# The state scan of a decoder layer laid out as 4 states x 32 channels on the partitions, with one scan instruction for a pair of rows and four sum strips

## The reference, cut to what matters

```
A  = -exp(A_log)                                   # 2048 x 16
dA = exp(dt_t[..., None] * A)                      # b, d, n
dBx = dt_t[..., None] * B_t[:, None, :] * x_t[..., None]
h  = dA * h + dBx
y  = einsum('bdn,bn->bd', h, C_t)
...
y  = (ys + D_param[None, :, None] * xc) * silu(z)
```

## Time and profile before

| what | value |
|---|---|
| median of 3 runs | 3586.15 us (3581.65 to 3586.78) |
| the profiled execution | 3582.83 us |
| its span, first to last instruction | 3581.5 us |
| the scan's DVE work | 446.3 to 1251.3 us of the span |
| DVE busy in that stretch | 791.2 of 804.9 us |
| POOL busy | 739.7 us |
| PE busy | 612.5 us |
| ACT busy | 358.2 us |
| mean granted TensorE clock in it | 0.95 |

### The profile page before, as it was taken

How to read it: one execution, slowest core, us unless ns; L and a number is a source line. 1 busy time by engine, 2 the same in 40 slices (tenths; PEclk the granted TensorE clock), 3 DMA queues, 4 the chain that set the end, 5 groups by cost and what they waited for, 6 DMA issues and landing times. The chain is left out here.

```text
span 3581.5 us, 41307 instructions
## 1 busy us (share of the span) xinstructions
PE 3221.2 (90%) x12763; PEld 2387.8 (67%) x12763; DVE 2195.0 (61%) x1925; ACT 1512.5 (42%) x2148; POOL 1399.2 (39%) x794
## 2 busy tenths in 40 slices
PE   9999777878777689999799999997889999999996
PEld 7877433333332267898587878786668888888884
DVE  6554499999999946621377777774644333333426
ACT  4447644444444432411387888782321122121111
POOL 0002299999999823000287878780100000000001
PEclk9999889999999999999899999999999999999998
DMA  3124531113110076422211111115211111111101
GB/s 110 41 80 165 184 128 62 45 50 139 50 62 31 15 252 208 144 80 94 76 32 32 35 31 35 31 33 199 78 65 47 41 59 53 35 53 53 47 18 59
DMA packets 125427, 273.15 MB, mean 76 GB/s; under 512 B 24448, under 2 KB 38656, under 8 KB 122400
## 3 DMA queue, kind: packets, MB, share of 16 engines
q1 hardware_dynamic: 107632, 262.42, 21.7%
q10 hardware_dynamic: 17712, 9.79, 0.9%
HBM read 207.87 MB, written 64.29 MB: 76 GB/s over the span
## 5 line engine op out<-in xcount | busy, mean ns | idle before, releaser
L799 PE MATMUL scan_ps_y<-scan_g,scan_ident 128*128 128x512 f32 x1024 | 518.8, 640 | 189.5 <-DVE scan_g L730 172.8
L771 POOL TENSOR_TENSOR scan_dbx<-scan_u,scan_b_bc 128x1024 f32<-128x1024 f32 x256 | 594.2, 2355 | 31.6 <-DMA scan_b_bc<-bc 31.6
L1552 POOL TENSOR_TENSOR at_p_lo<-at_p,at_p_hi 128x512 fp32r<-128x512 f32 x384 | 515.7, 1350 | 159.5 <-ACT at_p_hi L1458 149.1
L702 ACT ACTIVATE scan_ps_a<-scan_dt,scan_a_neg 128x512 f32<-128x512 f32 x512 | 328.0, 679 | 442.6 <-DVE scan_g L730 435.7
L799 PEld LDWEIGHTS scan_ps_y<-scan_g,scan_ident 128*128 128x128 f32 x1024 | 193.2, 199 | 482.5 <-DVE scan_g L730 296.0
L927 POOL TENSOR_TENSOR ff_y<-ff_y,ff_rstd 128x512 f32<-128x512 f32 x14 | 24.9, 1806 | 1124.1 <-DVE ff_rstd L916 1124.1
L743 DVE TENSOR_TENSOR_SCAN scan_ps_a<-scan_ps_a,scan_dbx 128x512 f32<-128x512 f32 x384 | 441.5, 1210 | 1.5 <-POOL scan_dbx L771 1.5
L1497 DVE TENSOR_REDUCE at_neg_max<-at_ps_mx 128x1 fp32r<-128x1536 f32 x132 | 232.0, 1758 | 164.3 <-PE at_ps_mx L1572 152.4
L1972 DVE TENSOR_TENSOR ff_hf<-ff_sg,ff_ps_u 128x1024 f32<-128x1024 f32 x28 | 34.2, 1221 | 388.2 <-PE ff_ps_u L97 388.2
L1455 ACT ACTIVATE at_p<-at_ps_s 128x512 f32<-128x512 f32 x384 | 227.8, 593 | 104.7 <-PE at_ps_s L1589 86.6
L1458 ACT ACTIVATE at_p_hi<-at_p 128x512 fp32r<-128x512 f32 x384 | 242.8, 632 | 12.2
(11 more groups left out here) (253 smaller groups left out, 7201.3 us busy)
## 6 DMA issues: line engine op xcount, KB each, us to landing
ff_w<-in_w SPq DMA_DIRECT2D x56, 512.0 KB, 4.2
in_w<-in_w_in SPq DMA_DIRECT2D x32, 512.0 KB, 3.6
mid_w<-in_w_out SPq DMA_DIRECT2D x32, 512.0 KB, 4.8
ff_w<-in_w SPq DMA_DIRECT2D x56, 256.0 KB, 2.6
ff_wo_wo<-in_w_o SPq DMA_DIRECT2D x32, 384.0 KB, 3.1
scan_cx<-in_ctx SPq DMA_DIRECT2D x9, 1024.0 KB, 5.7
sz<-in_xz SPq DMA_DIRECT2D x16, 512.0 KB, 3.0
dt<-in_acc SPq DMA_DIRECT2D x16, 512.0 KB, 3.6
```

The source lines that it names most:

```text
L702: nc.scalar.activation(ps_a[(2 * s + k) % SB][:, h], dt[s][:], ACT.Exp, scale=a_neg[:, it, 2 * k + h:2 * k + h + 1]).then_inc(a_ready, 1)
L771: nc.gpsimd.tensor_tensor(dbx[k % SL][:], u[s][:].unsqueeze(1).to_broadcast([P, 2, L]), b_bc[:, 2 * k:2 * k + 2], ALU.mult).then_inc(dbx_r ...
L799: last = nc.tensor.matmul(ps_y[:], ident[:], g[(2 * s + k) % SB][:, h], start=False, stop=k == NK - 1 and h == 1)
L1552: nc.gpsimd.tensor_tensor(p_lo[t % NSL][:], p[t % NSL][:], f32(p_hi[t % NSL][:]), ALU.subtract).then_inc(p_lo_done, 1)
```

## The change

The layout of the scan is turned: a tile now holds four groups of 32 partitions (`CG` = 4, `CW` = 32). Partition group `a` carries the states 4a to 4a+3, and the free dimension carries one position row for each of the four channel groups of 32 (`c`). A block is still 128 channels with 8 pairs, but a pair is now one of the four states of each group, for two channel groups.

- `b_bc` and `c_bc` hold 4 rows for each batch, both batches at once; they are read with a stride of zero over the two halves of a pair. `dt` and `u` are spread: each group of 32 partitions gets all four channel groups, so a load is four DMAs of 256 KB instead of one. Two tiles of each exist instead of three.
- The two scans of a pair become one of 128x1024. ACT writes the second half of the decays from its second position on and a zero into its first position, by a third, one-column activation; the scan runs over the boundary and starts anew there.
- The sum over the states of a partition group is done by a selection matrix `sel` of 128x32. For each two pairs (`t`, 128 of them) PE issues four matmuls, one for each channel group `c`, whose outputs are 32 partitions of `ps_y` each (strips). D * x is written by four strip matmuls as well. All four strips wait for both pairs.
- There are four `g` tiles. A wait for `summed` now means: the four strips that hold pairs n-4 and n-3 are done.
- `after` stands ahead of the decays of pair 3, the diagonal ahead of those of pair 6; the key matmuls are issued two behind each of 12 of 16 sums, through a bank that is copied alternately into two `kb` tiles.
- All loops are written out.

The diff, cut to its core:

```diff
     NIT = B * IT
+    CG = 4
+    CW = P // CG
+    NB = NS // CG
     NK = NS // 2
-    CH = 4
-    SL = 4
-    SB = 3
+    NP = NK * NIT
+    SL, SG, SA = 4, 4, 3
+    NSUM = NP // 2
     KW = KV * HD
     KF = KW // P
-    KC_TOK = 256
-    NC_B = CTX // KC_TOK
-    NKC = B * NC_B
-    NU = KF * NKC
-    assert KF == SB and NU <= NIT - 2
-    b_bc = sb("b_bc", [P, NS, L])
-    c_bc = sb("c_bc", [P, NS, L])
-    dbx = [sb(f"dbx{s}", [P, 2, L]) for s in range(SL)]
-    g = [sb(f"g{s}", [P, 2, L]) for s in range(SB)]
-    dt = [sb(f"dt{s}", [P, L]) for s in range(SB)]
-    u = [sb(f"u{s}", [P, L]) for s in range(SB)]
-    yb = [sb(f"yb{s}", [P, L]) for s in range(SB)]
-    a_neg = sb("a_neg", [P, NIT, NS])
-    a_exp = sb("a_exp", [P, NIT, NS])
-    d_p = sb("d_p", [P, NIT])
+    TOKS = 256
+    NCH = B * CTX // TOKS
+    BPC = NSUM // NCH
+    KPB = 2
+    b_bc = sb("b_bc", [P, B, NB, L])
+    c_bc = sb("c_bc", [P, B, NB, L])
+    dt = [sb(f"dt{s}", [P, CG, L]) for s in range(2)]
+    u = [sb(f"u{s}", [P, CG, L]) for s in range(2)]
+    dbx = [sb(f"dbx{s}", [P, 2 * L]) for s in range(SL)]
+    g = [sb(f"g{s}", [P, 2 * L]) for s in range(SG)]
+    yb = [sb(f"yb{s}", [P, L]) for s in range(2)]
+    a_neg = sb("a_neg", [P, IT, NS])
+    a_exp = sb("a_exp", [P, IT, NS])
+    d_p = sb("d_p", [P, IT])
     ident = sb("ident", [P, P])
-    d_diag = [sb(f"d_diag{s}", [P, P]) for s in range(SB)]
+    sel = sb("sel", [P, CW])
...
-    ps_a = [res.bank(f"scan_ps_a{s}", [P, 2, L]) for s in range(SB)]
+    ps_a = [res.bank(f"scan_ps_a{s}", [P, 2 * L]) for s in range(SA)]
     ps_y = res.bank("scan_ps_y", [P, L])
-    ps_k = res.bank("scan_ps_k", [P, KC_TOK])
+    ps_x = res.bank("scan_ps_x", [P, L])
...
+            def load_spread(tile, src, done):
+
+                for a in range(CG):
+                    sp.dma_start(tile[a * CW:(a + 1) * CW], src.rearrange("(c d) l -> d c l", c=CG)).then_inc(done, 16)
+
+            def load_rows(tile, b, row, done):
+
+                for a in range(CG):
+                    r = row + NB * a
+                    sp.dma_start(tile[a * CW:(a + 1) * CW, b], d["bc"][b, r:r + NB].partition_broadcast(CW)).then_inc(done, 16)
+
+            def load_dt(it):
+                load_spread(dt[it % 2], d["dt"][it], dt_ld[it % 2])
+
+            def load_u(it):
+                load_spread(u[it % 2], d["u"][it], u_ld[it % 2])
+
...
+            for it in range(NIT):
+                if it:
+                    store(it - 1)
                 if it + 2 < NIT:
-                    body(it, it % SB)
-                else:
-                    store(it - 1, (it - 1) % SB)
-            store(NIT - 1, (NIT - 1) % SB)
-            for s in range(SB):
-                sp.wait_ge(y_st[s], 16 * len(range(s, NIT, SB)))
-            sp.wait_ge(k_st, 16 * NU)
-            sp.wait_ge(cx_ld, 16 * (NKC + 1))
+                    sp.wait_ge(a_ready, 3 * NK * (it + 1))
+                    load_dt(it + 2)
+                    sp.wait_ge(dbx_ready, NK * (it + 1))
+                    load_u(it + 2)
+                c, last = divmod(it + 1, NIT // NCH)
+                if last == 0 and c < NCH:
+                    sp.wait_ge(k_mm, KF * c)
+                    load_chunk(c)
+            store(NIT - 1)
...
+            for n in range(NP):
+                it, k = divmod(n, NK)
+                if k == 0:
+                    act.wait_ge(dt_ld[it % 2], 16 * CG * (it // 2 + 1))
+                if k == 3 and it:
+                    after(it - 1)
+                for q in range(KF * NCH):
+                    if n == 2 * unit_end(q) + 6:
+                        store_keys(q)
+                if k == 6 and it + 1 < NIT:
+                    act.wait_ge(summed, CG * NB * it + CG)
+                    diagonal(it + 1)
+                if n >= SA:
+                    free_a(n - SA)
+                at = ps_a[n % SA]
+                for h in range(2):
+                    c = 2 * (k % 2) + h
+                    e = 2 * k + h
+                    nc.scalar.activation(at[:, h * L + h:(h + 1) * L], dt[it % 2][:, c, h:L], ACT.Exp,
+                                         scale=a_neg[:, it % IT, e:e + 1]).then_inc(a_ready, 1)
+                nc.scalar.activation(at[:, L:L + 1], ident[:, 0:1], ACT.Copy, scale=0.0).then_inc(a_ready, 1)
+            after(NIT - 1)
...
         @block.vector
         def _(dve):
-            def times_c(n, s, k):
-
-                dve.wait_ge(scanned, 2 * SL + 2 * n + 2)
-                dve.wait_ge(summed, n + 2)
-                nc.vector.tensor_tensor(g[s][:], ps_a[s][:], c_bc[:, 2 * k:2 * k + 2], ALU.mult).then_inc(g_ready, 1)
-
-            def body(it, s, chunk, tile):
-                first = isinstance(it, int) and it == 0
-                for k in range(NK):
-                    n = NK * it + k
-                    slot = (2 * s + k) % SB
-                    out = g[slot] if k in BY_POOL else ps_a[slot]
-                    dve.wait_ge(dbx_ready, n + 1)
-                    if k in BY_POOL:
-                        dve.wait_ge(summed, n + 2)
-                    for h in range(2):
-                        dve.wait_ge(a_ready, 2 * n + h + 1)
-                        nc.vector.tensor_tensor_scan(out[:, h], ps_a[slot][:, h], dbx[k % SL][:, h], 0.0,
-                                                     ALU.mult, ALU.add).then_inc(scanned, 1)
-                    if (k - 1) % NK in BY_POOL:
-                        continue
-                    if not first or k:
-                        if k % 2 == 1 or k % 4 == 2:
-                            dve.wait_ge(c_ld[(k - 1) // 2], 16 * (it // IT + 1))
-                        times_c(n - 1, (slot - 1) % SB, (k - 1) % NK)
-
-            dve.sem_inc(scanned, 2 * SL)
-            blocks(dve, body)
-            last = NIT - 1
-            times_c(NK * NIT - 1, (2 * last + NK - 1) % SB, NK - 1)
+            def times_c(n):
+
+                dve.wait_ge(scanned, n + 1)
+                if n >= SG:
+                    dve.wait_ge(summed, CG * ((n - SG) // 2 + 1))
+                nc.vector.tensor_tensor(g[n % SG][:].rearrange("p (h l) -> p h l", h=2),
+                                        ps_a[n % SA][:].rearrange("p (h l) -> p h l", h=2),
+                                        c_bc[:, n // (NP // B), n % NK // 2].unsqueeze(1).to_broadcast([P, 2, L]),
+                                        ALU.mult).then_inc(g_ready, 1)
+
+            for n in range(NP):
+                dve.wait_ge(dbx_ready, n + 1)
+                dve.wait_ge(a_ready, 3 * n + 3)
+                if by_pool(n) and n >= SG:
+                    dve.wait_ge(summed, CG * ((n - SG) // 2 + 1))
+                out = g[n % SG] if by_pool(n) else ps_a[n % SA]
+                nc.vector.tensor_tensor_scan(out[:], ps_a[n % SA][:], dbx[n % SL][:], 0.0, ALU.mult, ALU.add).then_inc(scanned, 1)
+                if n and not by_pool(n - 1):
+                    if n % (NP // B) == 2:
+                        dve.wait_ge(c_ld[n // (NP // B)], 16 * CG)
+                    times_c(n - 1)
+            times_c(NP - 1)
...
+            for n in range(NP):
+                it, k = divmod(n, NK)
+                b = it // IT
+                if k == 0:
+                    pool.wait_ge(u_ld[it % 2], 16 * CG * (it // 2 + 1))
+                    pool.wait_ge(b_ld[b], 16 * CG)
+                if n >= SL:
+                    pool.wait_ge(scanned, n - SL + 1)
+                c = 2 * (k % 2)
+                nc.gpsimd.tensor_tensor(dbx[n % SL][:].rearrange("p (h l) -> p h l", h=2), u[it % 2][:, c:c + 2],
+                                        b_bc[:, b, k // 2].unsqueeze(1).to_broadcast([P, 2, L]),
+                                        ALU.mult).then_inc(dbx_ready, 1)
+                if n >= BEHIND and by_pool(n - BEHIND):
+                    times_c(n - BEHIND)
...
+            pe.wait_ge(par_ld, 16 * 4)
+            for t in range(NSUM):
+                it, m = divmod(t, NB)
+                if m == 0:
+                    if it:
+                        pe.wait_ge(epi_done, it)
+                    pe.wait_ge(diag_done, it + 1)
+                    for c in range(CG):
+                        strip = slice(c * CW, (c + 1) * CW)
+                        nc.tensor.matmul(ps_y[strip], d_diag[it % 2][:, strip], xc[:, it], start=True, stop=False)
+                wait_product(2 * t)
+                wait_product(2 * t + 1)
+                for c in range(CG):
+                    h = c % 2
+                    nc.tensor.matmul(ps_y[c * CW:(c + 1) * CW], sel[:], g[(2 * t + c // 2) % SG][:, h * L:(h + 1) * L],
+                                     start=False, stop=m == NB - 1).then_inc(summed, 1)
+                c, at = divmod(t, BPC)
+                for i in range(KPB * at, min(KPB * (at + 1), KF * HT)):
+                    key_product(c, i)
...
-        "a_log": a[m + "A_log"].reshape(IT, P, NS).transpose(1, 0, 2),
```

(68 more changed lines are left out.)

149 lines of the change are left out of this document (33 added, 116 removed).

## The result

The changed kernel takes 3565.30 us (median of 4, 3563.01 to 3566.46), the one before in the same comparison 3585.92. The ratio is 0.9943 with a 95% interval of 0.9927 to 0.9959: 0.6% faster, where 3675 was predicted. Run again beside later kernels it gave 0.9947 (0.9934 to 0.9961).

A forecast was written before the change was run, and what follows sets the result against it. DVE's stream was taken to bound the scan: 25.2 + 858.7 + 1.1 + 6.9 gave 891.9 us against 804.9, +87.0; start +1 and end +1 gave 3672, and the median's 3.3 made 3675, range 3557 to 3735.

The forecast's parts named there:

- PE's sums: DVE waits for packets of four strips on PE, priced serially at 3.44 us, done after 3.70; 3.45 us added a block.
- The signs named as wrong: Scan's strip passes starting well under 0.43 us apart; mean clock well below 0.95; scans near 2.4 us; longer ACT waits.
- The chain around it: In each block DVE loses 0.5 us at pair 3, 2.4 at scan 4, 0.55 at the next block's scan 0.
- rival 3: Serial strips and falling PE clock in the scan: 1.5 us more a block, 3721 us in all; chance 0.12.
- The price of a pass: On PE each pass of 512 columns takes 0.43 us, from 3.60 - 1.88 between eight and four passes.
- Rival 1: Strips overlap on PE and DVE's wait never bites: stage 778 us, 3560 us in all; chance 0.23.
- rival 2: Strips overlap but PE's clock falls in the scan: 1.7 us more a block, 3612 us in all; chance 0.20.
- The merge: Two DVE scans become one, saving 0.06 us a pair (bounds nothing and 0.15), 15 us over the stage.
- Waits: DVE's 12.8 us of waits in the old scan: first block's 5.9 need not return, 6.9 kept.
- The start: Before the scan SP issues 12 DMAs before `u` is complete, instead of three before B: +1 us.
- ACT's third activation: One-column activation for each pair on ACT: between nothing and 0.39 us; a pair's decays taken as 1.5 us, fitting the cover.
- Loops written out: Scan loops written out: no row shows a cost, the 4.4 us issue wait occurs once at the start; nothing.

The follow-up runs named there:

- the one-strip run: The changed kernel with all four matmuls of a packet written into the same strip, weights still 128x32: 3690.26 us, ratio 1.0293 to the kernel before.
- wide strips: The changed kernel with every packet matmul writing all 128 partitions; D * x as four full matmuls: 3743.97 us; as one: 3677.44 us.

## Why the prediction was wrong

The step that failed is the price in *PE's sums*: "I take the upper, since every row of this trace has PE's passes one behind the other". Four strips take 1.06 us at full clock, just under the lower bound named there (0.86 and 0.26, or 1.12), not 3.70. So the 3.45 us of lost time a block do not arise; 31 blocks of them are 107 us, nearly the whole distance of 110 between forecast and result. The rows could not settle it: no row of before wrote to separate strips, and passes with 128 columns of weights do run one behind the other, as the one-strip run shows for narrow ones too. The signs named as wrong came true: passes that start together, and a mean granted clock of 0.65. "Nearest row" was no evidence on a property that the nearest row doesn't have.

*The chain around it* was right in its places (wide strips: pair 3 for ACT, pairs 4 and 0 for PE) and too small in size, since the packet before `after` falls to half clock there. Even with serial strips 3675 would not have come: the run built that way took 3744, above rival 3's 3721 as well. *The price of a pass*, 0.43 us, was right, though the 1.88 that it was worked out with is not in the earlier trace rows, which show 1.98; eight passes end after 3.60 us, not 3.70.

*Rival 1* is what happened: 3560 worked out, 3565 measured. Its 778 us for the stretch against 778.4 is partly luck: a block was 24.26 us instead of 24.16, which is 3 us more in all, and the small waits were 1.7 us instead of 4. The 5 us that it missed are about what it had too little at the start. Its condition, four strips in at most 2.6 us, is met even at half clock (1.94). That is why *rival 2* was half right: the clock fell, to 0.65 on average, and cost DVE 0.3 us. The Trainium skill, "TensorE: Matmul & The Clock Gate", Part 3 (packing small matmuls), says that strips run concurrently, and the trace agrees. My reading of it, that only the second pass of a strip can run beside the next strip's first (five pass times), was too cautious: the first passes of all four strips run together, then the second ones, two pass times. The key matmuls between the strips cost no visible stop either: the first key pass starts at 610.44, when the packet begun at 609.45 is just ending.

*The merge*: 0.06 us a pair taken, 0.05 measured (2.24 to 2.19), 13 us; shown from both sides, by undoing it (11.6 to 17 us) and by making it alone (13 us).

*Waits*: 12.8 us in the old scan are 1.7 now, 11 us; of this the prediction had counted only the first block's 5.9. Of these, 1.5 were for a part of B, which is now there before the first scan. The profile names no releaser for the other 4.4; they end at 463.7, about when PE is through with the sums of pairs 0 and 1, eight passes that begin at 457.09 and run at half clock. Which part of the change takes the others away, the strips' speed or the fourth `g` tile, no run on the new layout separates; in the old layout a fourth `g` tile alone does it (9.1 us of waits for PE to none).

*The start*: +1 taken, +7.5 measured. I priced twelve issues and one landing time; the DMA engines are full from 440 to 451, and 3 MB at 223 GB/s are 14 us. The term was missing a bandwidth.

*ACT's third activation* takes 0.15 us, inside its bounds and hidden. *Loops written out*: nothing, as taken. The sum of the measured parts is -13 (merge), -11 (waits) and +7.5 (start), together -16.5 against -20.6 measured. The other 4 us I can't place beyond gaps of DVE and the shorter tail (7.7 us instead of 9.9 between the last product and the next phase).

## What to carry to other kernels

The price of a packet of work that another engine waits for depends on whether its parts can run side by side. Where the trace has no such part, work out both bounds in full, and don't take one as the likelier only because its row is nearest in shape. Then find the longest packet that other work still hides (here 2.6 us by the prediction's sum). It lay between the two bounds (1.12 and 3.70), so one price that no row gave decided the result. Try a part of a change by itself as well: the merged scan and a fourth `g` tile in the old layout gave all of the time. And when a start or a wait is mended, look at what is queued next: 8 us won at the start came to nothing until the key matmuls, which waited for a late load in front of the sums, were moved.

## What the runs showed of the hardware

- Four f32 matmuls of 128x32 weights and 512 columns to four different strips of 32 partitions: 1.06 us together at full clock, 1.94 at half. To one and the same strip: 3.62 us.
- One 128x1024 scan costs 2.19 us from start to start, two of 128x512 cost 2.24; a one-column activation lasts 0.15 us.
- With the DMA engines full, loads that each write 32 partitions moved 223 GB/s, while loads that each write 128 moved 427 in the kernel before. Packets of one size took twice as long to 32 partitions (8 KB: 0.60 us for 0.31; 2 KB: 0.16 for 0.08), so the row length does not explain it.
- The mean granted clock of PE was 0.65 over the changed scan, and DVE waited 0.3 us for PE in it: the lower clock cost nothing here, where DVE's own work hid the packets.
